# Expert layer: the second product of a block as one matmul of 512 and one of 256 columns, with a y bank per expert and three banks in turn for the hidden layer

## The reference, cut to what matters

```
gate_logits = einsum('bsd,de->bse', x, Wg) + bg
top_vals, top_idx = top_k(gate_logits, 2);  gate_scores = softmax(top_vals)
for i in range(2):
    e = top_idx[..., i].reshape(-1)[:batch]        # one expert for each sequence
    h = gelu(einsum('bsd,bdh->bsh', x, W1[e]) + b1[e])
    y = einsum('bsh,bhd->bsd', h, W2[e]) + b2[e]
    out = out + gate_scores[..., i:i+1] * y
```

## Time and profile before

| | |
|---|---|
| median of 3 runs | 4155.37 us |
| the profiled execution's own time | 4155.98 us |
| its span, first to last instruction | 4154.1 us |
| TensorE busy | 3900.6 us, 94% of the span |
| weight loads | 3097.8 us, 75% |
| VectorE, ScalarE, GpSimd busy | 3005.8, 2199.1, 2147.2 us |
| expert layer, first to last matmul | about 983 to 2644 us |

### The profile page before, as it was taken

The page is one execution under the profiler, slowest core; times in us unless marked ns, Lnnn a source line. Parts: engine busy times, 40 slices in busy tenths (PEclk is TensorE's granted clock), DMA queues, the critical chain, the costliest instruction groups (busy, mean ns, idle before and its releaser), DMA issues. The chain is left out here.

```text
span 4154.1 us, 140077 instructions
## 1 busy us (share of the span) xinstructions
PE 3900.6 (94%) x49269; PEld 3097.8 (75%) x49456; DVE 3005.8 (72%) x5010; ACT 2199.1 (53%) x4529; POOL 2147.2 (52%) x3316
## 2 busy tenths in 40 slices
PE   6999999975999999999999999699989997999999
PEld 4777777754888888888888888456656666888888
DVE  5888888866666666666666666489978985777777
ACT  3777777755333333333333333267767774555554
POOL 5666666652333322222222222346656666788777
PEclk9999999987999999999999999799999998999999
DMA  4677777745222222222222222489999973322322
GB/s 129 193 206 206 221 217 218 205 133 161 68 68 68 64 58 58 58 58 58 58 58 58 58 58 58 89 175 212 213 206 215 212 189 86 74 75 75 77 77 72
DMA packets 834262, 502.95 MB, mean 121 GB/s; under 512 B 262037, under 2 KB 824408, under 8 KB 833480
## 3 DMA queue, kind: packets, MB, share of 16 engines
q1 hardware_dynamic: 832680, 493.49, 46.9%
q0 software_dynamic: 928, 0.49, 0.1%
HBM read 251.27 MB, written 214.96 MB: 112 GB/s over the span
## 5 line engine op out<-in xcount | busy, mean ns | idle before, releaser
L1485 ACT ACTIVATE all_region<-phase_loop_hid,phase_b1T 128x128 f32<-128x128 f32 x2048 | 584.5, 368 | 1006.6 <-PE phase_loop_hid L186 1005.1
L184 PE MATMUL phase_loop_hid<-phase_loop_moe_h,phase_w_hi 128*128 128x128 f16 x4096 | 841.3, 224 | 3.2
L186 PE MATMUL phase_loop_hid<-phase_loop_moe_h,phase_w_lo 128*128 128x128 f16 x4096 | 824.8, 219 | 0.0
L185 PE MATMUL phase_loop_hid<-phase_loop_moe_h,phase_w_hi 128*128 128x128 f16 x4096 | 824.7, 219 | 0.0
L1503 DVE TENSOR_SCALAR all_region<-all_region 128x512 f16<-128x512 f32 x512 | 287.5, 561 | 592.1 <-ACT all_region L1485 589.6
L1095 DVE TENSOR_REDUCE phase_loop_mx<-phase_loop_score 128x8 f32<-128x1024 f32 x512 | 625.3, 1221 | 103.9 <-PE phase_loop_score L858 96.8
L1013 ACT ACTIVATE phase_loop_pt<-phase_loop_scoreT 128x1024 f32<-128x1024 f32 x448 | 458.2, 1023 | 269.5 <-PE phase_loop_scoreT L892 267.1
L1452 PE MATMUL phase_loop_moe_y<-phase_w,all_region 128*128 x2048 | 562.5, 275 | 3.6 <-issue 0.4
L1453 PE MATMUL phase_loop_moe_y<-phase_w,all_region 128*128 x2048 | 562.7, 275 | 0.0
L1454 PE MATMUL phase_loop_moe_y<-phase_w,all_region 128*128 x2048 | 558.2, 273 | 0.0
L184 PEld LDWEIGHTS phase_loop_hid<-phase_loop_moe_h,phase_w_hi 128*128 x4096 | 395.5, 97 | 145.0 <-issue 10.5
(11 more groups left out here) (266 smaller groups left out, 9537.3 us busy)
## 6 DMA issues: line engine op xcount, KB each, us to landing
qk_scratch<-phase_loop_qk SPq DMA_DIRECT2D x192, 256.0 KB, 3.6
phase_loop_qS<-qk_scratch SPq DMA_DIRECT2D x768, 64.0 KB, 3.3
phase_loop_cin<-in_ctx SPq DMA_DIRECT2D x128, 256.0 KB, 4.8
x_scratch<-phase_loop_x SPq DMA_DIRECT2D x128, 256.0 KB, 3.1
h_scratch<-phase_loop_hr SPq DMA_DIRECT2D x128, 256.0 KB, 3.9
phase_loop_kS<-qk_scratch SPq DMA_DIRECT2D x384, 64.0 KB, 2.4
ks_scratch<-ct_scratch SPq DMA_DIRECT2D x384, 64.0 KB, 2.4
phase_loop_kS<-ks_scratch SPq DMA_DIRECT2D x128, 192.0 KB, 3.9
```

The lines of the kernel that those rows point to most:

```text
L184: eng.matmul(out, l_hi, r_hi, start=start, stop=False)
L185: eng.matmul(out, l_hi, r_lo, start=False, stop=False)
L186: return eng.matmul(out, l_lo, r_hi, start=False, stop=stop)
L1485: i = act.activation(hf[n % NF][:, j, :], hid_bank[n % 4][:, j * S:(j + 1) * S], ACT.Gelu, bias=w["b1"][:, bass.ds(e * HB + (4 * half + j) ...
```

## The change

Each j of `down` makes two matmuls in place of three: `hh` against the whole `row`, 512 columns, and `hl` against its first 256 columns, added to the first half of the same bank. The parts hh x W2 hi and hh x W2 lo then lie side by side in a full bank for each sequence and expert (`y_bank[a][ex]`, four banks), and `add(a)` sums them with four VectorE operations in place of two. The hidden layer has three banks in turn, `hid_bank[(u.no * NC + n) % 3]`, and `up(n)` waits for `gelu(n - 3)`.

```diff
-        hid_bank = [k.ps(f"hid{i}") for i in range(4)]
-
-        y_bank = [k.ps(f"moe_y{a}") for a in range(PAIR)]
+        NB = 3
+        hid_bank = [k.ps(f"hid{i}") for i in range(NB)]
+
+        def hid(u, n):
+            return hid_bank[(u.no * NC + n) % NB]
+
+        y_bank = [[k.ps(f"moe_y{a}{ex}") for ex in range(2)] for a in range(PAIR)]
...
-        s_t, s_x2 = k.sig("m_t", 3 * PAIR), k.sig("m_x2", PAIR)
+        s_t, s_x2 = k.sig("m_t", 5 * PAIR), k.sig("m_x2", PAIR)
... up(n)
                         if n == 0:
                             d_h.wait(pe, u)
-
+                        s_ge.wait(pe, u, n + 1 - NB)
...
-                                m = three_passes(pe, hid_bank[n % 4][:, j * S:(j + 1) * S],
+                                m = three_passes(pe, hid(u, n)[:, j * S:(j + 1) * S],
... down(n)
-                        o = y_bank[a][:, ex * D:(ex + 1) * D]
+                        o = y_bank[a][ex]
                         for j in range(4):
                             row = w["w2"][:, bass.ds(e, 1), 4 * half + j, :, :].rearrange("p o t n -> p (o t n)")
-                            high, low = hh[n % NH][:, j, :], hl[n % NH][:, j, :]
-                            pe.matmul(o, high, row[:, 0:D], start=n % 4 == 0 and j == 0, stop=False, skip_group_check=True)
-                            pe.matmul(o, high, row[:, D:2 * D], start=False, stop=False, skip_group_check=True)
-                            m = pe.matmul(o, low, row[:, 0:D], start=False, stop=n % 4 == 3 and j == 3, skip_group_check=True)
+                            pe.matmul(o[:, :], hh[n % NH][:, j, :], row, start=half == 0 and j == 0, stop=False,
+                                      skip_group_check=True)
+                            m = pe.matmul(o[:, 0:D], hl[n % NH][:, j, :], row[:, 0:D], start=False,
+                                          stop=half == 1 and j == 3, skip_group_check=True)
... add(a)
-                        for ex in range(2):
-                            to, done = (at, s_t) if ex == 0 else (x2[u.slot][:, a, :], s_x2)
-                            s_t.wait(v, u, 3 * a + ex + 2)
-                            v.scalar_tensor_tensor(out=to, in0=y_bank[a][:, ex * D:(ex + 1) * D], scalar=weight(u, a, ex),
-                                                   in1=at, op0=ALU.mult, op1=ALU.add).then_inc(done.sem, 1)
+                        for i in range(4):
+                            ex, part = i // 2, i % 2
+                            to, done = (at, s_t) if i < 3 else (x2[u.slot][:, a, :], s_x2)
+                            s_t.wait(v, u, 5 * a + i + 2)
+                            v.scalar_tensor_tensor(out=to, in0=y_bank[a][ex][:, part * D:(part + 1) * D],
+                                                   scalar=weight(u, a, ex), in1=at,
+                                                   op0=ALU.mult, op1=ALU.add).then_inc(done.sem, 1)
```

More of the change, by code:

```diff
@@ L1484, in go @@
                         for j in range(4):
-                            i = act.activation(hf[n % NF][:, j, :], hid_bank[n % 4][:, j * S:(j + 1) * S], ACT.Gelu,
+                            i = act.activation(hf[n % NF][:, j, :], hid(u, n)[:, j * S:(j + 1) * S], ACT.Gelu,
                                                bias=w["b1"][:, bass.ds(e * HB + (4 * half + j), 1)],
@@ L1541, in go @@
                             if ex:
-                                s_t.wait(v, u, 3 * a + ex)
+                                s_t.wait(v, u, 5 * a + ex)
                             v.scalar_tensor_tensor(out=at, in0=w["b2"][:, bass.ds(e_now[2 * a + ex] * D, D)],
```

## The result

The changed kernel takes 3896.64 us (median of 4 runs, 3890.9 to 3904.39) against 4155.52 us for the kernel before on the same chip: a ratio of 0.9379, 95% interval 0.936 to 0.9398. It is 259 us faster; 3905 us was predicted, in a range of 3872 to 3956.

A forecast was written before the change was run, and what follows sets the result against it. TensorE's sequencer, making addresses by register steps, was taken to bound the expert layer. 3.84 + 0.2 - 0.1 = 3.94 us a unit over 64 units, 252 us, less some 3, gave 3905 us, range 3872 to 3956.

The forecast's parts named there:

- The bound: Expert layer: TensorE's sequencer, making addresses between matmuls, sets the pace, 4.3 us a unit above the engine.
- The register step: Down blocks: one FUSED_REGOPS a j left of two, 32 a unit removed at 0.12 us, saving 3.84 us.
- the 3 us taken off for the start and the end of the layer: Some 3 us less saving, for the half-clock start and the last down blocks with no up behind them.
- The instructions around it: About 800 instructions a unit become 700, so an eighth of 1.6 us of irregular extras goes: 0.2 us.
- The wait: up(n) on gelu(n - 3): holds nothing, rides on the first matmul; only up(0) pays, 0.1 us (0 to 0.3).
- The lead: Sequencer gets 0.8 us ahead in a down block, falls back 0.6 to 0.7 in up; the lead carries across.
- a short queue: Rival: TensorE's queue holds only a lead of four groups, so down's saving is lost; 4151 us, chance 2%.
- a slow engine: Rival: a 128-column matmul with weight load costs 0.072 us on TensorE, up stays at 1.72; 4151 us, chance 4%.
- eight priced waits: Rival: each of the eight new waits costs a 0.18 us step, giving back 92 us; about 3997 us, chance 7%.
- the rival of two addresses: Rival: down's two operands don't share an address, so 8 FUSED steps a block stay; about 4153 us, chance 4%.
- Two limits that meet: Per unit: sequencer 22.0 us, engine floor 21.6; the range's high bound let them hinder each other by 0.6 us.
- VectorE: Four more adds a unit, about 2.0 us, hidden; 3.3 us of waiting left. Rival, VectorE becomes the bound: slower, 3%.

The follow-up runs named there:

- experiment 1: Kernel before with the second down matmul (L1453) reading the same 256 columns as the first, dropping its register step, all matmuls kept: 3900.15 us, ratio 0.9387.
- experiment 2: Changed kernel with the second matmul of each j reading the other 256 columns of row, so the register steps return: 4160.93 us, ratio 1.0014.
- experiment 3: Changed kernel with the 512-column matmul cut into two of 256; banks, wait and adds kept: 4164.85 us, ratio 1.0025.
- experiment 4: Kernel before with only three hidden-layer banks in turn and up(n) waiting for gelu(n - 3): 4165.57 us, ratio 1.0026.
- experiment 9: Changed kernel with one hidden-layer bank instead of three, so up(n) waits for gelu(n - 1): 4327.3 us, ratio 1.0415.
- experiment 8: Changed kernel with L186 reading the same w1_hi piece as L184 and L185, so each group's ALU_OP falls away: 3878.29 us, ratio 0.9336.
- experiment 7: Changed kernel with one TensorE TENSOR_LOAD of expert numbers for two units, same result: 3882.0 us, ratio 0.9346.
- experiment 6: Changed kernel with two adds in place of four in add(a), leaving out the W2_lo half of y: 3897.07 us, ratio 0.9381.

## Why the prediction was right

**The bound.** That the sequencer sets the pace was read from two paces of one matmul shape and from the list of register instructions. Experiments 1, 2 and 3 show it from both sides: the step without the matmul gives the whole gain, the matmul without the step about 4 us.

**The register step.** 0.12 us was read from timelines rounded to 0.01. The start times of the register instructions in the traces give it directly: from a FUSED_REGOPS to the next register instruction most steps take 0.124 us, from an ALU_OP 0.112 to 0.113, before and after the change. So the 32 steps a unit are 3.97 us, not 3.84. Over 2048 steps this is 8 us, and the forecast was 8 us too high (3905 against 3896.64). That the two match so well is partly luck: the forecast already had 1 us for this, the two smaller terms below were together 0.07 us a unit too favourable, and the 3 us taken off for the start and the end of the layer do not show in the 259 us between the TENSOR_LOADs. It is luck too that experiment 1 gives 0.124 from the whole time: its layer saved 263 us, extras included, and the rest of the profiled execution was 9 us longer.

**The instructions around it.** I took 0.2 us a unit for an eighth of the irregular extras. The start times settle that the term exists. The time of the register steps above 0.124 and 0.1125 us adds up to 1.52 us a unit before the change and 1.36 after it, 0.16 less. It goes more with the register instructions than with the matmuls, as experiment 1, which removes only the former, has 1.37 and experiment 2, which removes only the latter, 1.48. What the extras are (0.28 us in some groups where 0.237 is usual) is open, and no kernel here tried it.

**The wait.** Taken at 0.1 us a unit, measured at 0.13 (experiment 4). The other seven are free. The prediction had them ride on the first matmul of the block; they stand on the first register step, which costs as little while gelu is done early and matters in experiment 9.

**The lead.** The sequencer's lead is carried over a whole up block, as the first unit of the kernel before had suggested: all up blocks but up(0) run at 0.056 us throughout, and even the TENSOR_LOAD is hidden, at up(0)'s expense. In the changed kernel a FUSED_REGOPS of `up` runs up to 1.4 us ahead of its matmul; in the kernel before it was 0.43 at most. The rivals of a short queue, of a slow engine and of eight priced waits fall with that and with experiments 1 and 4; the rival of two addresses falls with the count of 2048.

The rule of the Trainium skill ("TensorE: Matmul & The Clock Gate", "Back-to-back issue gap") of about 81 ns for a matmul of 128 columns with its weight load came close to the average before (1.72/24 = 72 ns). The changed kernel disagrees with it: 24 such pairs in 1.34 us, 56 ns each, the weight loads included.

**Two limits that meet.** Forecast: sequencer 22.0, engine 21.6. Measured: 21.89 together, and 21.46 for the engine alone (experiment 8). The difference of 0.43 us is lost in the first up block of a unit (1.74 against 1.34 us, all other blocks being the same); experiment 7 gets 0.25 of it back by a shorter and rarer load. The two limits do not hinder each other, as the high bound had allowed for: the register steps take no longer than before (0.124 and 0.113 us, with fewer extras), so nothing holds the sequencer, and 21.89 is its own time.

**VectorE.** Covered, as forecast, and shown by experiment 6.

## What to carry to other kernels

When one shape of matmul shows two paces at the same clock, look for the sequencer: count the register instructions between the matmuls and price one where the engine is starved. An address that depends on a register costs a step each time that a new offset is made from it, so lay data out to let one address serve several instructions; an untouched part of the program may get the gain. A wait cost nothing here when what it waits for was done early, but where the sequencer runs ahead to pay for such steps, a wait that holds up the matmuls by 0.2 us cost 0.85 us a block.

## What was not expected of the hardware

The wait of a block stands on the register step that makes its first address, so an open one stops all register steps behind it (experiment 9): 0.2 us of direct delay a block, 6.8 us a unit in all. And a TENSOR_LOAD of eight numbers from one row took 0.591 us at the median, where one of six took 0.817 (experiment 7). I don't know why.
